# Two float32r pieces in place of three bfloat16 pieces, and the vector engine's input work on other steps

## The reference, cut to what matters

```python
def _div_clamp_fp8(x, scale):
    y = jnp.clip(x.astype(jnp.float32) / scale, -FP8_MAX, FP8_MAX)
    y = y.astype(jnp.bfloat16).astype(jnp.float32)
    return _fp8_roundtrip(y)
def _fp8_linear_pertensor(x, wq, w_scale, in_scale):
    xq = _div_clamp_fp8(x, in_scale)
    return jnp.einsum('bsi,oi->bso', xq * in_scale, wq) * w_scale
...
ln_out = _ln(hidden_states, ln_w, ln_b)
q = _fp8_linear_pertensor(ln_out, wq, wq_scale, q_in_scale).reshape(b, s, g, hpg, d)
q = _ln(q, qln_w, qln_b)
k = _fp8_linear_pertensor(ln_out, wk, wk_scale, k_in_scale).reshape(b, s, g, d)
k = _ln(k, kln_w, kln_b)
v = _fp8_linear_pertensor(ln_out, wv, wv_scale, v_in_scale).reshape(b, s, g, d)
core = _gqa(q, k, v).reshape(b, s, nh * d)
qx = _fp8_linear_pertensor(ln_out, wqx, wqx_scale, qx_in_scale).reshape(b, s, g, hpg, d)
...
kvx = jnp.einsum('bsi,oi->bso', cond, w_kv_x)
...
xout = _gqa(qx, kx, vx).reshape(b, s, nh * d)
cat = jnp.concatenate([core, xout], axis=-1)
catq = _div_clamp_fp8(cat, proj_smooth)
return jnp.einsum('bsi,oi->bso', catq, wproj) * (proj_in_scale * proj_w_scale)
```

## Time and profile before

| | us |
|---|---|
| median of 3 runs | 1890.98 |
| lowest and highest of the 3 runs | 1885.7 and 1893.93 |
| span of the profiled execution | 1885.4 |
| first instruction of the stage's work, to its last step | about 561 to 1030 |
| first matmul of the stage's products | 570.65 |

### The profile page before, as it was taken

How to read it: one execution, slowest core, us unless ns; L and a number is a source line. 1 busy time by engine, 2 the same in 40 slices (tenths; PEclk the granted TensorE clock), 3 DMA queues, 4 the chain that set the end, 5 groups by cost and what they waited for, 6 DMA issues and landing times. The chain is left out here.

```text
span 1885.4 us, 29601 instructions
## 1 busy us (share of the span) xinstructions
PE 1590.0 (84%) x9245; PEld 1122.1 (60%) x9326; DVE 1338.5 (71%) x3795; ACT 834.7 (44%) x2405; POOL 620.1 (33%) x750
## 2 busy tenths in 40 slices
PE   4898898695447999999897799998978999799984
PEld 3443344463224666666675688887854555788872
DVE  6799797798866888889887347566454333478876
ACT  3133454474534677667675233332331221344451
POOL 1300020675216788788784310111120001221000
PEclk9899999798668999999999899999989999899996
DMA  4255300200909100000000600000162222523200
GB/s 161 63 149 180 112 1 1 84 2 9 166 28 357 59 1 2 1 1 1 1 1 1 206 11 22 18 12 12 35 202 97 85 90 76 190 90 104 72 28 12
DMA packets 103592, 129.36 MB, mean 69 GB/s; under 512 B 14160, under 2 KB 89136, under 8 KB 99984
## 3 DMA queue, kind: packets, MB, share of 16 engines
q1 hardware_dynamic: 94448, 112.39, 18.5%
q0 software_dynamic: 8992, 15.08, 3.8%
HBM read 85.75 MB, written 46.94 MB: 70 GB/s over the span
## 5 line engine op out<-in xcount | busy, mean ns | idle before, releaser
L2464 PE MATMUL l2fa_psQ<-l2fa_xT,l2f_home 128*128 128x128 f32 x1024 | 123.8, 281 | 0.9 <-DMA l2f_home<-in_L2f_kvT 0.9
L2464 PEld LDWEIGHTS l2fa_psQ<-l2fa_xT,l2f_home 128*128 128x128 f32 x1024 | 120.7, 197 | 3.2 <-issue 1.6
L588 POOL TENSOR_TENSOR l0f_diag<-g_identb,l0f_mask 128x1024 bf16<-128x1024 bf16 x16 | 31.9, 2021 | 210.0 <-PE l0f_psA L879 191.6
L2961 ACT ACTIVATE l2x_probs<-l2x_psS,l2x_nmax 128x128 f32<-128x128 f32 x256 | 90.8, 376 | 15.0 <-DVE l2x_nmax L2880 14.9
L3247 POOL TENSOR_TENSOR route_rrms<-route_vrms,g_minus_half 128x1 f32<-128x1 f32 x8 | 5.7, 706 | 267.3 <-DVE route_vrms L3269 267.3
L2782 POOL TENSOR_TENSOR l2x_probs<-l2x_probs,l2x_rtotal 128x512 f32<-128x512 f32 x64 | 66.5, 1038 | 71.1 <-DVE l2x_rtotal L2886 71.1
L3832 POOL DMA_INDIRECT routed_rows<-rows,route_slot_of x32 | 31.4, 982 | 177.1 <-DMA rows<-moe_yg 168.4
L2791 POOL TENSOR_TENSOR l2x_vsm<-l2x_vraw,l2x_smooth_row 128x512 f32<-128x512 f32 x64 | 88.4, 1381 | 0.0
L3656 DVE COPY moe_xgT<-moe_psX 128x256 f32<-128x256 f32 x47 | 20.0, 425 | 92.7 <-PE moe_psX L3762 92.7
L3106 PEld LDWEIGHTS l2x_psS<-l2x_kT,l2x_qT 128*128 128x128 f32 x512 | 66.3, 191 | 23.9 <-issue 19.7
L1547 ACT ACTIVATE l2fa_probs<-l2fa_psS,l2fa_bias 128x128 f32<-128x128 f32 x128 | 45.2, 365 | 76.7 <-DVE l2fa_bias L1531 76.7
(11 more groups left out here) (564 smaller groups left out, 4643.9 us busy)
## 6 DMA issues: line engine op xcount, KB each, us to landing
rows<-l2x_zero SPq DMA_DIRECT2D x1, 18304.0 KB, 60.4
kT_ctx<-l0f_held SPq DMA_DIRECT2D x32, 256.0 KB, 3.5
v_ctx<-l0f_held SPq DMA_DIRECT2D x32, 256.0 KB, 3.6
...
```

What stands on the lines that cost most here:

```text
L2464: last = nc.tensor.matmul(psQ[bank][:, j, :], w[:, c, h * HD:(h + 1) * HD], xT[u][:, c, :], start=(c == 0), stop=(c == KC - 1))
L2961: last = nc.scalar.activation(probs[:, n % 2, j, :], psS[:, j, :], ACT.Exp, bias=nmax[:, n % 2, j:j + 1], scale=1.0, accum_out=total[:, n ...
```

## The change

Two things are changed together.

1. The four weights become float32r in SBUF (a 4-byte format; the load from float32 is a DMA from POOL's queue as before, with twice the bytes written). `whole` is split into two float32r pieces: one cast on ACT (`keep_high_part`), one pair of subtractions on POOL (`keep_low_part`). A projection is 2 pieces x 2 blocks = 4 matmuls.
2. The input work moves. On DVE, `variance` goes from step 6 to step 4, `norm` from step 0 to step 6 of the sequence before, `clip` from step 2 to step 0, `up` stays at step 2, `round` goes from step 3 to step 2, `apply_scales` stays at step 4, now behind `variance`. For sequence 1, `variance` and `norm` stand ahead of the first step. On POOL, the subtraction stays at step 5, `invert` goes from step 6 to step 5 behind it, `scale` from step 1 to step 7; `keep_last_part` at step 7 is gone. On ACT the second cast at step 6 is gone.

To find room, tiles share memory: `pT` of an earlier stage lies in `wkv`, its neighbour's `h` in a weight buffer, and `scaled` and `clipped` are two halves of `whole`; `xa` is gone. No instruction is added for that.

```diff
-        self.wq, self.wqx = T.sb("wq", [P, KC, S1], BF16), T.sb("wqx", [P, KC, S1], BF16)
-        self.wk, self.wv = T.sb("wk", [P, KC, S2], BF16), T.sb("wv", [P, KC, S2], BF16)
+        self.wq, self.wqx = T.sb("wq", [P, KC, S1], F32R), T.sb("wqx", [P, KC, S1], F32R)
+        self.wk, self.wv = T.sb("wk", [P, KC, S2], F32R), T.sb("wv", [P, KC, S2], F32R)
...
-        part = [T.sb(f"part{u}", [P, 3, 4 * KC, P], BF16) for u in range(2)]
+        part = [T.sb(f"part{u}", [P, 2, 4 * KC, P], F32R) for u in range(2)]
...
-                def take_first_part(b):
+                def keep_low_part(b):
                     pool.wait_ge(hi_ready, b + 1)
                     for j in range(0, 8, 4):
-                        nc.gpsimd.tensor_tensor(whole[:, j:j + 4, :], whole[:, j:j + 4, :], part[b % 2][:, 0, j:j + 4, :],
-                                                ALU.subtract).then_inc(rest_ready, 1)
-
-                def keep_last_part(b):
-                    pool.wait_ge(mid_ready, b + 1)
-                    for j in range(0, 8, 4):
-                        nc.gpsimd.tensor_tensor(part[b % 2][:, 2, j:j + 4, :], whole[:, j:j + 4, :],
-                                                part[b % 2][:, 1, j:j + 4, :], ALU.subtract).then_inc(parts_ready, 1)
+                        nc.gpsimd.tensor_tensor(part[b % 2][:, 1, j:j + 4, :], whole[:, j:j + 4, :],
+                                                part[b % 2][:, 0, j:j + 4, :], ALU.subtract).then_inc(parts_ready, 1)
...
-                    if b + 1 < B and i == 7:
-                        keep_last_part(b + 1)
...
-                    if t == 0:
-                        I.invert(pool, G, 1)
-                    elif i == 6 and b + 2 < B:
-                        I.invert(pool, G, b + 2)
-                    if b + 1 < B:
-                        if i == 1:
-                            I.scale(pool, b + 1, W.in_row)
-                        elif i == 5:
-                            take_first_part(b + 1)
+                    if b + 1 < B and i == 5:
+                        keep_low_part(b + 1)
+                    if b + 2 < B:
+                        if i == 5:
+                            I.invert(pool, G, b + 2)
+                        elif i == 7:
+                            I.scale(pool, b + 2, W.in_row)
...
-                take_first_part(0)
-                keep_last_part(0)
+                keep_low_part(0)
+                I.invert(pool, G, 1)
+                I.scale(pool, 1, W.in_row)
...
-                    if t == 0:
-                        I.variance(dve, G, 1)
-                    elif i == 6 and b + 2 < B:
-                        I.variance(dve, G, b + 2)
+                    if b + 2 < B:
+                        if i == 4:
+                            I.variance(dve, G, b + 2)
+                        elif i == 6:
+                            I.norm(dve, G, W, b + 2)
                     if b + 1 < B:
                         if i == 0:
-                            I.norm(dve, G, W, b + 1)
+                            I.clip(dve, b + 1)
                         elif i == 2:
-                            I.clip(dve, b + 1)
                             I.up(dve, b + 1)
-                        elif i == 3:
                             I.round(dve, b + 1)
                         elif i == 4:
                             apply_scales(b + 1)
...
                 apply_scales(0)
+                I.variance(dve, G, 1)
+                I.norm(dve, G, W, 1)
                 steps(one)
...
                     return [(part[b % 2][:, r, source * KC + c, :], w[:, c, col:col + 512])
-                            for r in range(3) for c in range(KC)]
+                            for r in range(2) for c in range(KC)]
```

More of the change, by code:

```diff
@@ L18 @@
 BF16 = mybir.dt.bfloat16
+F32R = mybir.dt.float32r
 I32 = mybir.dt.int32
@@ L926, in sum, with stage_l1_xattn @@
                 .then_inc(self.summed, 1)
-def stage_l1_xattn(nc, G, A, V):
+def stage_l1_xattn(nc, G, A, V, W):
     with ExitStack() as ctx:
@@ L1196, in stage_l1_ffn @@
         sil = T.sb("sil", [P, H1])
-        h = [T.sb(f"h{u}", [P, H1]) for u in range(2)]
+        h = [w[0][:, u * H1:(u + 1) * H1] for u in range(2)]
         hh = T.sb("hh", [P, 2])
@@ L2620, in __init__ @@
         self.ve, self.rstd = T.sb("ve", [P, 1]), T.sb("rstd", [P, 1])
-        self.xa, self.xn = T.sb("xa", [P, D]), T.sb("xn", [P, D])
-        self.scaled, self.clipped = T.sb("scaled", [P, 4, D], BF16), T.sb("clipped", [P, 4, D], BF16)
+        self.xn = T.sb("xn", [P, D])
+        self.whole = T.sb("whole", [P, 4 * KC, P])
+        half = lambda j: self.whole[:, 4 * j:4 * j + 4, :].rearrange("p k t -> p (k t)").bitcast(BF16)\
+            .rearrange("p (j d) -> p j d", j=4)
+        self.scaled, self.clipped = half(0), half(1)
         self.magic, self.raised = T.sb("magic", [P, 4, D], BF16), T.sb("raised", [P, 4, D], BF16)
@@ L2640, in norm @@
         nc = self.nc
-        self.o.step(nc.vector.scalar_tensor_tensor(out=self.xa[:, :], in0=G.x[:, b, :], scalar=self.mv[:, 0:1],
+        wait(dve, self.scaled_ready, 2 * b)
+        self.o.step(nc.vector.scalar_tensor_tensor(out=self.xn[:, :], in0=G.x[:, b, :], scalar=self.mv[:, 0:1],
                                                    in1=W.lnw[:, :], op0=ALU.subtract, op1=ALU.mult))
         dve.wait_ge(self.x_rstd, b + 1)
-        wait(dve, self.scaled_ready, 2 * b)
-        nc.vector.scalar_tensor_tensor(out=self.xn[:, :], in0=self.xa[:, :], scalar=self.rstd[:, :], in1=W.lnb[:, :],
+        nc.vector.scalar_tensor_tensor(out=self.xn[:, :], in0=self.xn[:, :], scalar=self.rstd[:, :], in1=W.lnb[:, :],
                                        op0=ALU.mult, op1=ALU.add).then_inc(self.xn_ready, 1)
@@ L2681, in stage_l2_xattn @@
         xq = I.xq
-        whole = T.sb("whole", [P, 4 * KC, P])
-        part = [T.sb(f"part{u}", [P, 3, 4 * KC, P], BF16) for u in range(2)]
+        whole = I.whole
+        part = [T.sb(f"part{u}", [P, 2, 4 * KC, P], F32R) for u in range(2)]
         hstats = T.sb("hstats", [P, 2, 4, 6])
@@ L2945, in _, with keep_high_part @@
             def _(act):
-                def keep_first_part(b):
+                def keep_high_part(b):
                     act.wait_ge(whole_ready, b + 1)
@@ L2950, in keep_first_part @@
                     nc.scalar.copy(part[b % 2][:, 0, :, :], whole[:, :, :]).then_inc(hi_ready, 1)
-                def keep_middle_part(b):
-                    act.wait_ge(rest_ready, 2 * (b + 1))
-                    nc.scalar.copy(part[b % 2][:, 1, :, :], whole[:, :, :]).then_inc(mid_ready, 1)
                 def exponentials(n):
@@ L3028, in one @@
                         if i == 5:
[L3029 to L3031 removed]
+                            keep_high_part(b + 1)
                 act.wait_ge(W.consts_made, W.CONSTS)
[L3034 to L3035 removed]
+                keep_high_part(0)
                 steps(one)
@@ L3167, in stages_l1_l2_xattn @@
             V = TernaryWeights(nc, held)
-            stage_l1_xattn(nc, G, A, V)
+            stage_l1_xattn(nc, G, A, V, W)
             stage_l1_ffn(nc, G, A, W, V, I)
```

10 lines of the change are left out of this document (2 added, 8 removed).

## The result

The changed kernel takes 1871.47 us (median of 4 runs, 1868.86 to 1874.61), the kernel before beside it 1891.45: a ratio of 0.9899, 95% interval 0.9881 to 0.9917.

The account below looks back on a forecast made before the run. DVE was taken to set the pace, PE mattering only where DVE waits for it on even steps. The entry's -6.4 us and -2 us over six sequences gave -8.5 us, carried to the median: 1882.5 us, range 1872 to 1898.

Parts of the forecast that it names:

- the collision at step 2: DVE's input work at step 2: POOL's `vsm` delays a long instruction, so it takes 2.9 us, bounds 1.8 and 3.1.
- the entry: Start of the stage: PE starts earlier, fewer cold matmuls, input work moved; -6.4 us, bounds -4.5 and -7.5.
- the dips: Clock falls at some step 3 while PE waits for late DVE; a shorter step 2 removes some, 0.4 us a sequence.
- Rival (a): Step 2 doesn't collide: a sequence gains 1.2 us and the clock dips mostly go; 1875.5 us, chance 0.28.
- Step 4: `variance` is new ahead of `apply_scales` on DVE, with no wait left to hide in: +0.74 us a sequence.
- Steps 3, 6 and 0: Moved `round` (step 3), `norm` for `variance` (6), `clip` for `norm` (0): each put at 0 us a sequence.
- Step 0: The 0.43 us key wait gain is lost to the POOL and ACT chain, started late by `scale`: 0, bounds -0.2 and +0.3.
- A float32r matmul: PE's time for one float32r matmul, taken as 0.216 us, with bounds 0.216 and 0.86.
- (c): All 12 products of a sequence: a float32r matmul runs at the 0.43 us of a float32 record; 1912 us, chance 0.09.
- (d): All 12 products of a sequence: float32r runs like float32, 0.86 us a matmul; over 2080 us, chance 0.03.
- Rival (b): POOL becomes what DVE waits for, through `scale` at step 7 and `invert` at step 5; 1888.5 us, chance 0.15.
- The last step: Carrying the -8.5 us against the profiled execution's 1885.4 us over to the median of 1890.98: 1882.5 us.

Follow-up runs that it names:

- one_bias_op: The changed kernel with one of POOL's two small query bias instructions moved to ACT, where ACT waits; 1865.5 us, ratio 0.9864 to the kernel before.
- pieces_only: The changed kernel's two float32r pieces, with input work in the old steps of the kernel before; 1876.1 us, ratio 0.993 to the kernel before.
- two_bf16: The changed kernel with bfloat16 in place of float32r for pieces and weights; 1868.3 us, ratio 0.9872 to the kernel before.
- moves_only: The changed kernel with three bfloat16 pieces as before, input work in the new steps; 1909.4 us, ratio 1.0099 to the kernel before.

## Why the prediction came out as it did

**The step that failed is the collision at step 2**, the term "I take 2.9" between its bounds of 1.8 and 3.1. It measured 1.79. The rule behind it (who is issued first) was right; the moment was wrong. `vsm` was put 4.66 us behind POOL's normalising, as in the earlier trace rows, and it came 5.19 behind. POOL starts its chain earlier against DVE now (normalising 0.22 us behind the start of the reciprocal, 0.54 before), and its small instructions take longer: `qrstd` 1.14 instead of 1.01, `qbias` 0.40 instead of 0.20, and from the start of `krstd` to `vsm` 1.27 instead of 1.01. With 4.66, `vsm` would have come at 857.83, in the first long instruction, as in one_bias_op. So 1-2 and 2-3 together gave 1.63 us a sequence where 0.6 was forecast, 6.2 us over six sequences.

The stage shrank by 6.3 us more than the 8.5 forecast. That this is the same number is luck in part: the entry gave 3.0 less than forecast, while the dips (1.5), the irregular step of before (1.2) and the first sequence gave more. Outside its entry the stage shrank by 11.4 us, which the prediction itself had named as a sign of being wrong (over 10).

Rival (a) had this mechanism, and its 1875.5 lies just inside the interval of the result (up to 1875.8). Its terms were off and made up for each other: 1.2 us a sequence, where its own rows give 0.94 (1.25 and 0.43 less 0.74) and 0.78 was measured; 6.4 for the entry, where 3.4 was measured; and 0.2 to 0.4 a sequence for the dips, where 3.9 in all went. With a margin of 0.3 us between it and the forecast, its chance of 0.28 was too small.

**What was right in a sequence.** Step 4: +0.74 forecast, +0.77 measured. Steps 3, 6 and 0: nothing, and 0.00, -0.02, +0.10. Waits for the key product: 0.41 at steps 0 and 2 (0.34 forecast), 1.20 at step 4, 1.05 at step 6.

**Step 0.** The gain in the key wait is lost to the chain through POOL and ACT, as forecast, and `scale` makes normalising start 0.34 us later there (0.3 to 0.4 forecast). But `scale` isn't needed for it: pieces_only has the same 6.67 us without it, since POOL's small instructions take as much longer. In the kernel before the chain was already within 0.1 us of DVE at this step, so that a shorter key wait could bring next to nothing. "DVE sets the pace, PE matters only where DVE waits for it" was therefore half the truth: in pieces_only the key waits fall by 1.08 us a sequence and the sequence by 0.56.

**Mis-sized.** A float32r matmul: 0.26, not 0.216; by two_bf16 that costs 0.3 us a sequence. The entry: -3.4 and -5.6 in two executions, -6.4 forecast; PE's start was nearly right (-3.2 against `apply_scales`, -3.5 forecast); the rest differs between the two executions, along with the stretches of low granted clock. The dips: 0.4 a sequence forecast, 2.4 in all; all 3.9 us went.

**Rivals (c) and (d)** fell with the train of 0.26. **Rival (b)** is what moves_only does: without the shorter POOL work of two pieces, the same moves lose 19 to 20 us.

**The last step**, from the profile to the median, did not hold. It carried the same change over to the median; but the profiled execution of before was its lowest of four, that of after its highest, and their spans are 12.7 us apart, the stages 14.8 (16.6 with the second profile of after), the medians 20. With the stage's 14.8 to 16.6 alone the time would have been 1875 to 1877. Where the other 3 to 5 us lie stays open.
